# First expert layer: rows loaded in 32-column blocks and turned on VectorE, the last normalisation two groups later

## The reference, cut to what matters

```python
xt = x.reshape(-1, Hd)                        # 8192 x 128, normalised
probs = softmax(xt @ Wr + br)                 # 8 experts
gate, idx = max(probs), argmax(probs)
h1 = relu(xt @ W1[e] + b1[e])                 # 128 -> 512
ye = h1 @ W2[e] + b2[e]                       # 512 -> 128
y  = ye[idx] * gate
```

## Time and profile before

| | |
|---|---|
| median of 3 runs | 1828.78 us (1828.15 to 1830.52) |
| the profiled execution's own time | 1829.2 us |
| its span | 1827.4 us |
| PE busy | 1661.5 us (91%) |
| DVE busy | 1170.4 us (64%) |
| ACT busy | 1007.3 us (55%) |
| POOL busy | 824.3 us (45%) |
| mean granted TensorE clock | 0.958 |
| expert stage of layer 0 | from about 853 to 1007 us of the span |

### The profile page before, as it was taken

The page is one execution under the profiler, slowest core; times in us unless marked ns, Lnnn a source line. Parts: engine busy times, 40 slices in busy tenths (PEclk is TensorE's granted clock), DMA queues, the critical chain, the costliest instruction groups (busy, mean ns, idle before and its releaser), DMA issues. The chain is left out here.

```text
span 1827.4 us, 44219 instructions
## 1 busy us (share of the span) xinstructions
PE 1661.5 (91%) x14314; PEld 1239.0 (68%) x14315; DVE 1170.4 (64%) x2727; ACT 1007.3 (55%) x2546; POOL 824.3 (45%) x1414
## 2 busy tenths in 40 slices
PE   4799999999999999998999499999999999995783
PEld 4655666666555566665899388888888888884672
DVE  3356555555555555553444399999999999996661
ACT  3344555555555555553344377877778777772341
POOL 6234444444444444454343544444444444422663
PEclk9999999999999999999999699999999999996776
DMA  8313112222122222222222111121111111215434
GB/s 220 95 21 65 38 37 41 43 43 42 41 43 43 43 43 43 43 46 59 62 66 61 24 41 43 39 45 38 41 42 40 41 42 40 43 36 106 96 80 115
DMA packets 193767, 100.11 MB, mean 55 GB/s; under 512 B 99313, under 2 KB 185138, under 8 KB 190514
## 3 DMA queue, kind: packets, MB, share of 16 engines
q1 hardware_dynamic: 183474, 85.81, 20.9%
q0 software_dynamic: 10240, 13.64, 3.5%
HBM read 65.00 MB, written 38.06 MB: 56 GB/s over the span
## 5 line engine op out<-in xcount | busy, mean ns | idle before, releaser
L641 POOL TENSOR_SCALAR_AFFINE_SELECT probs<-probs 128x512 f32<-128x512 f32 x256 | 174.5, 705 | 198.7 <-ACT probs L1422 198.6
L1422 ACT ACTIVATE probs<-bankT 128x1024 f32<-128x1024 f32 x128 | 131.2, 1025 | 220.9 <-PE bankT L1774 216.6
L878 DVE TENSOR_REDUCE mneg<-bankS 128x2 f32<-128x256 f32 x256 | 109.1, 426 | 213.8 <-PE bankS L1754 212.1
L879 DVE TENSOR_REDUCE mneg<-bankS 128x2 f32<-128x512 f32 x256 | 174.8, 683 | 0.0
L1413 ACT ACTIVATE qT<-bankA,bd 128x256 f32<-128x256 f32 x256 | 107.6, 473 | 90.9 <-PE bankA L1736 90.9
L1736 PE MATMUL bankA<-xnT,wd 128*128 128x256 f32 x512 | 149.8, 416 | 0.0
L634 POOL CAST qb<-qT 128x256 bf16<-128x256 f32 x256 | 97.2, 398 | 98.8 <-ACT qT L1413 98.6
L1788 PE MATMUL bankB<-probs,vaug 128*64 128x512 f32 x512 | 139.8, 625 | 1.1 <-ACT yT L1429 1.0
L1771 PE MATMUL bankT<-qT,kT 37*128 37x512 f32 x512 | 137.0, 611 | 3.0 <-ACT probs L1424 1.8
L1222 DVE STREAM_TRANSPOSE pt<-pe 128x768 f32<-128x768 f32 x128 | 123.7, 967 | 0.3 <-ACT pe L1518 0.2
L1518 ACT ACTIVATE pe<-pr 128x768 f32<-128x768 f32 x128 | 108.1, 844 | 28.3 <-DVE pr L1216 26.1
(11 more groups left out here) (316 smaller groups left out, 4605.3 us busy)
## 6 DMA issues: line engine op xcount, KB each, us to landing
rzb<-reciprocals SPq DMA_DIRECT2D x64, 384.0 KB, 5.3
xtab<-tab SPq DMA_DIRECT2D x32, 192.0 KB, 2.0
xs_sorted<-zeros SPq DMA_DIRECT2D x1, 4608.0 KB, 19.2
qT<-xs_sorted SPq DMA_DIRECT2D x36, 128.0 KB, 2.1
ys_sorted<-qT SPq DMA_DIRECT2D x36, 128.0 KB, 1.8
value_rows<-vrow SPq DMA_DIRECT2D x32, 128.0 KB, 1.8
vx<-value_rows SPq DMA_DIRECT2D x256, 16.0 KB, 1.8
acc<-res SPq DMA_DIRECT2D x32, 128.0 KB, 1.9
```

Of the source, the lines that this page charges most:

```text
L641: pool.affine_select(out=blocks, in_=blocks, compare_op=ALU.is_ge, fill=0.0, base=0, pattern=[[0, 4], [1, P]], channel_multiplier=-1).then ...
L878: dve.tensor_reduce(mneg[:, n.half, 0, :, j], bankS[:, :, 0:128], AX.X, ALU.max, negate=True)
L879: dve.tensor_reduce(mneg[:, n.half, 1, :, j], bankS[:, :, 128:384], AX.X, ALU.max, negate=True).then_inc(S["red_done"], 1)
L1422: act.activation(pT[:, g % 2].rearrange("p e j t -> p e (j t)"), bankT[:, 0:2, :], ACT.Exp, scale=SCALE0).then_inc(S["exp_done"], 1)
```

## The change

1. A load of two tiles becomes four loads, one for each 32 channels. Load k puts channels 32k to 32k+31 of the 256 rows on partitions 32k to 32k+31: row 32m + r of the tiles goes to partition 32k + r, at block m. Each moves 256 pieces of 128 bytes.
2. `turn_in` leaves PE and goes to DVE: one `dve.transpose` of 128 x 128, which turns each 32 x 32 block in place and so gives the whole turned tile, from `xsb` to `xsT` directly. PE's turning pass and ACT's copy are gone. Banks A and B are no longer used for it. DVE's order in a tile step is `turn_in` of tile j+2, `hidden` of tile j+1, `result` of tile j, as PE's was.
3. SP's loads wait for `xsT_sb` (turned by DVE) where they waited for `xsT_ps` (turned by PE).
4. `normalise(last, q)` stands behind the tiles of group 3 and no longer behind those of group 1; groups 2 and 3 are written out and the loop starts at 4.

```diff
             def load(i, u):
-                sp.dma_start(xsb[:, u], xs_d[bass.ds((i * 2 + u) * 2 * P, 2 * P), :].rearrange("(t p) c -> p t c", p=P)).then_inc(S[f"xs_in{u}"], 16)
+                for k in range(C // W):
+                    sp.dma_start(xsb[W * k:W * (k + 1), u].rearrange("r t (n c) -> r (t n) c", c=W),
+                                 xs_d[bass.ds((i * 2 + u) * 2 * P, 2 * P), W * k:W * (k + 1)].rearrange("(m r) c -> r m c", r=W)).then_inc(S[f"xs_in{u}"], 16)
...
             with sp.Fori(1, TILES // 4 - 1) as i:
                 for u in range(2):
-                    sp.wait_ge(S["xsT_ps"], i * 4 + (2 * u + 2))
+                    sp.wait_ge(S["xsT_sb"], i * 4 + (2 * u + 2))
                     load(i + 1, u)
                     store(i, u)
...
+            def turn_in(i, q):
+                j, i, q = i * 4 + q, i + q // 4, q % 4
+                if q % 2 == 0:
+                    dve.wait_ge(S[f"xs_in{q // 2}"], i * 64 + 64)
+                passed(dve)
+                dve.transpose(xsT[:, q % 2, :], xsb[:, q // 2, q % 2, :]).then_inc(S["xsT_sb"], 1)
+
             def tile_step(i, q, left):
                 j = i * 4 + q
+                if left > 2:
+                    turn_in(i, q + 2)
                 if left > 1:
                     hidden(j + 1, q + 1)
                 result(i, q)
...
             for q in range(4):
                 tile_step(1, q, 8)
+            for q in range(4):
+                tile_step(2, q, 8)
+            for q in range(4):
+                tile_step(3, q, 8)
                 normalise(last, q)
-            with dve.Fori(2, TILES // 4 - 1) as i:
+            with dve.Fori(4, TILES // 4 - 1) as i:
...
-            def turned(j, q):
-                act.wait_ge(S["xsT_ps"], j + 1)
-                act.copy(xsT[:, q % 2, :], bank[q % 2][:, 0:P]).then_inc(S["xsT_sb"], 1)
...
-            def turn_in(i, q):
-
-                i, q = i + q // 4, q % 4
-                if q % 2 == 0:
-                    pe.wait_ge(S[f"xs_in{q // 2}"], i * 16 + 16)
-                passed(pe)
-                pe.transpose(bank[q % 2][:, 0:P], xsb[:, q // 2, q % 2, :], ident[:, :]).then_inc(S["xsT_ps"], 1)
```

More of the change, by code:

```diff
@@ L416, in _ @@
             denominators_out(last)
-            sp.wait_ge(S["xsT_ps"], 2)
+            sp.wait_ge(S["xsT_sb"], 2)
             load(1, 0)
@@ L420, in _ @@
             reciprocals_out(last)
-            sp.wait_ge(S["xsT_ps"], 4)
+            sp.wait_ge(S["xsT_sb"], 4)
             load(1, 1)
@@ L1121, in _ @@
                 dve.sem_inc(S[f"ys_out{u}"], 16)
+            turn_in(0, 0)
+            turn_in(0, 1)
             hidden(0, 0)
@@ L1496, in tile_step @@
             def tile_step(j, q, left):
-                if left > 2:
-                    turned(j + 2, q + 2)
                 if left > 1:
                     hidden(j + 1, q + 1)
-            turned(0, 0)
-            turned(1, 1)
             hidden(0, 0)
@@ L1649, in columns @@
             def columns(g):
-                act.wait_ge(S["xsT_ps"], TILES + g + 1)
+                act.wait_ge(S["xsT_ps"], g + 1)
                 act.copy(xgT[:, g % 2, :], turn_ps).then_inc(S["xsT_sb"], 1)
@@ L1936, in tile_step @@
                 j = i * 4 + q
-                if left > 2:
-                    turn_in(i, q + 2)
                 if left > 1:
@@ L1944, in tile_step @@
                 result(j, q)
-            turn_in(0, 0)
-            turn_in(0, 1)
             hidden(0, 0)
```

## The result

| | before | after |
|---|---|---|
| median | 1829.65 us (1828.15 to 1830.55, 4 runs) | 1818.82 us (1817.6 to 1822.17, 4 runs) |
| ratio | | 0.9945, interval 0.9927 to 0.9962 |
| profiled execution | 1829.2 us, span 1827.4 | 1822.17 us, span 1820.5 |
| stage: start of the sum ahead of it to start of the sum at its end | 852.91 to 1007.54: 154.63 us | 856.14 to 1001.12: 144.98 us |
| four tiles in the loop, mean from 890 to 985 us | 8.04 us | 7.53 us |

The change is faster by 10.8 us in the medians and by 9.65 us in the stage that it touches. The profiled execution of the change reached the stage 3.23 us later than that of before, through work that the change does not touch, so its own time lies above its median; from here on the stage is compared, not the span.

What follows compares the result with a forecast made beforehand. TensorE was busy 19.58 of 20 us; after the change a buffer's cycle through loads and store was to set the pace. Terms -2.5 - 3.15 + 0.2 = -5.45 us gave 1823.3 us, range 1817.5 to 1833.

Steps and rivals of the forecast that it cites:

- my likeliest case: Whole kernel: the loop's buffer cycle takes 7.70 to 7.96 us for four tiles, total 1821 to 1825; chance 0.39.
- the first rival: Loop: TensorE keeps the pace at 7.61 us, the buffer cycle taking only 7.49; total 1818.0 us, chance 0.18.
- the pitch: SyncE's loop: time between two load issues, 0.45 to issue plus 0.21 for registers, 0.66 us.
- TensorE's own pace: Loop: without its turning passes of 0.11 us each, TensorE alone would take 7.61 us for four tiles.
- The ring: Loop: one buffer's way from store through four loads, turn, hidden layer and add to its next store, 7.85 us.
- The other buffer: Loop: the buffer whose load follows its store by 0.61 instead of 0.95 us takes 7.51, so sets no pace.
- TensorE idle a little for VectorE's transpose: Loop: a sign expected in the profile after the change, TensorE waiting briefly for the turned tile; no size given.
- -3.15 us: Loop from the add of tile 8 on: 63 tiles, 15.75 fours, each saving 8.05 - 7.85 = 0.20 us.
- VectorE's turn at nothing, 302 ns: Tile step: VectorE's 128x128 transpose takes 302 ns and by itself costs nothing, fitting where VectorE idled 0.78 us.
- the slower rival: Loop: loads land 2.8 us after issue, the buffer cycle takes 8.70 us; total 1836.7 us, chance 0.18.
- The reciprocals, "-2.5 us": Stage up to tile 8, start included: 3.9 us gained at full clock, less 1.4 for the slow clock.
- The normalisation's "+0.2": Groups 2 and 3: normalisation's multiplications beside VectorE's turn, 1.89 of 1.96 us a tile, charged 0.2 us.

Runs made afterwards that it cites:

- one load: The change with one load of 128 x 2 x 128 in place of four, rows wrong but work the same: stage 139.11 us, median 1814.74, ratio 0.9917.
- five loads: The change with the first of its four loads split in two, same bytes: stage 150.92 us, median 1823.93 us, ratio 0.9977.
- ahead: The change with SyncE's loads issued ahead of the stores, and tile 8's and 9's ahead of the reciprocals: stage 134.86 us, median 1807.83, ratio 0.989.
- old_ahead: The kernel before (TensorE turns, one load), normalisation behind group 3, SyncE's loads ahead of the stores: stage 149.70 us, median 1824.21, ratio 0.997.
- the repetition: The change itself once more, unaltered, on the same chip: stage 146.27 us, median 1817.0 us, ratio 0.9938 to the kernel before.

## Why the prediction was right, and where it was not

The direction and the range held: faster, 1818.8 inside 1817.5 to 1833. The time lies outside the band of my likeliest case, 1821 to 1825.5, and next to the first rival's 1818.0; but it got there by my case's mechanism, not by the rival's. That it still lies in the range is partly luck: the range's lower end came from that rival, and two sizes below were off, the pitch and TensorE's own pace. With the pitch alone put right, my own rule would have let TensorE's 7.61 set the pace.

- **The ring sets the pace: right.** Shown by one load (7.15), five loads (8.01) and the loads ahead (7.15), against 7.53. The rival "TensorE keeps the pace" is out.
- **"Sum: 0.95 + 1.98 + 1.95 + 0.50 + 2.28 + 0.19 = 7.85": the term that failed in size is the pitch.** The rows give 0.98; 1.83 - 0.32 = 1.51 for the three pitches; 941.22 to 943.13 = 1.91 for landing and wake; 0.31 for the turn; 0.21 to TensorE; 945.84 + 0.29 - 943.65 = 2.48; 0.20: 7.60 in this turn of the ring, 7.53 in the mean. The pitch is 0.50 and not 0.66: a load of 32 partitions is issued in 0.32 us, less than the 0.38 of the old one, while I had taken the value load's 0.45; and 0.19 are left for the registers. That is -0.47. Landing and VectorE's wake were 0.14 too dear, the turn with TensorE's wake 0.12 too cheap. In the other direction I had taken 0.11 off between the hidden layer and the add for a pass that never lay between them, and the piece took 0.09 more besides; the branch's 0.98 and the last 0.20 add 0.04.
- **The other buffer "is no bound": not contradicted.** VectorE waits for its load too (0.47 us before the transpose at 946.60), but TensorE takes that tile up only at 947.65, 0.74 us after it is turned.
- **"TensorE idle a little for VectorE's transpose": it didn't show.** The profile puts down only two waits of TensorE to the transposes, 4.1 us together, at the stage's start and at the reciprocals. In the loop the ring shows in late starts and, in most turns, a gap of about 0.2 us.
- **"-3.15 us" for the 63 tiles: -7.88 was measured**, 0.50 a four and not 0.20. This is nearly the whole difference between the forecast and the result.
- **"If TensorE alone set the pace, four tiles would take 7.61": wrong, 7.15.** I priced the turning pass at its 0.11 us in the queue. The gap of 0.45 us once in four tiles, which I had put down to the loop's branch and so left in, goes with it. It did not hurt the sum, as the ring stood above; it would have with a shorter ring, and it is why the load's place in the queue is worth another 0.38 a four.
- **VectorE's turn at nothing, 302 ns: right** (303). It is not free in time, it is free in place: 11.79 of 20 us busy. The rule of the Trainium skill, "VectorE: DVE Perf Modes", "Rules for kernel authors", that a 128x128 tile is turned on TensorE if its result may go to PSUM (the banks), would have kept the old kernel here. The trace speaks against it for this case: `old_ahead` and `ahead` differ in the turn and its loads alone, with 149.70 and 134.86 us.
- **Small pieces and their landing: the slower rival is out.** Landing is 1.7 in the median, below the old load's 2.1. The DMA engines were busy for 0.33 of the time at 67 GB/s where they were 0.23 at 66, so a piece of 128 bytes does cost more engine time a byte; the Trainium skill, "DMA: Bandwidth & Descriptors", "Specifications", puts line rate at 512 bytes and more, and the trace agrees in the share. It decides nothing here, as the engines are idle for two thirds.
- **The reciprocals, "-2.5 us": -1.77 to tile 8.** The turn behind the small loads started 874.04 - 866.42 = 7.62 after the reciprocals' issue, where I had 7.2, and from TensorE's start at 874.47 to the end of tile 8's add it took 5.76, where I had 4.2 and 1.4 for the slow clock. In the repetition nothing is gained up to tile 8 (25.56 against 25.57), so this term lies between 0 and -1.8.
- **The normalisation's "+0.2"** was not measured by itself; its move is worth 1.75 to 3 with the new turn, by single profiles that scatter by 1.3, and nothing without.

## What to carry to other kernels

Follow a buffer around through every queue that it passes before you judge a transfer by its size: here four small loads cost 0.38 us in four tiles only because they stood behind a store that they didn't need, and turning two lines of the queue gave all of it back, and most of the wait at the reciprocals with it. A pass on a full engine can cost more than its own width in the order of time, here 0.61 to 0.88 us for four of 0.11; take it out, or put an idle one in, and look at the loop. And where an engine shows as busy in both kernels, count its instructions in the stretch; its busy share may not tell them apart.

## What the runs showed of the hardware that was not expected

- A DMA of 32 partitions x 8 pieces of 128 bytes is issued in 0.32 us and lands in 1.7, against 0.38 and 2.1 for 128 partitions x 2 pieces of 512 bytes with four times the bytes; in a loop the issues stand 0.50 us apart.
- The turn on TensorE, one pass of 0.11 us per tile with its wait and ScalarE's copy, costs 0.88 us in four tiles (8.03 against 7.15) with no late load; an idle pass with nothing waiting for it costs 0.61 (one execution).
- TensorE's busy time was 19.99 of 20 us with 172 passes and 20.00 with 182, both at full granted clock.
- Small loads issued behind 768 KB of another transfer in the same queue were there only 7.62 us after the issue of the large ones; alone they land 1.7 us after their own. From 870 to 874 us the share of the DMA engines was 1.06, at 154 GB/s, so the runs don't tell the place in the queue from the full engines.
